# Pair sums of a Strassen-like down projection moved from accumulating DMAs to GpSimd, with new instruction orders around the stage

## The chip, the cores and the metric

One core of a Trainium2 chip runs the whole kernel. The metric is the device time of one execution in microseconds, as the median of the runs shown; lower is better. TensorE does the matmuls, VectorE (DVE), ScalarE (ACT) and GpSimd (POOL) the elementwise work, SyncE (SP) starts most DMAs.

## The reference, cut to what matters

```python
# x: 8 x 128 x 512 fp32 (1024 tokens), one LoRA index per batch row
gate = x @ W_gate.T + lora_gate(x)            # F = 1376, rank 16, scale 0.5
up   = x @ W_up.T   + lora_up(x)
act  = silu(gate) * up
c    = act @ W_down.T + lora_down(act)        # "first down projection", 512 out
nx   = c * rsqrt(mean(c*c) + 1e-5) * ln_w     # RMS norm
out  = x + (silu(nx @ g.T) * (nx @ u.T)) @ d.T   # I = 1792
```

## The kernel before

Every fp32 product is made of three fp32r matmuls: high part by high part, low by high, high by low. For each operand ACT writes the high part (a copy that rounds) and DVE then the low part (operand minus high part). So each operand costs one ACT copy and one DVE subtraction before TensorE may read it.

The large products are done in Winograd's form of Strassen's scheme: 2 x 2 blocks, seven products instead of eight, with sums of blocks as operands. The first down projection has the products 11, t2, 21, t3, t4, t1, 22, in this order on TensorE. `CDOWN` gives each its PSUM banks. Each has five items (`KC`), an item being three matmuls for each of two output tiles; 30 matmuls of 128 x 512 a product. The act operands of t2, t3, t4 and t1 are pair sums, made in place in the act buffer `act[:, tile, token half]`:

- t3: second half of tiles 0 to 4, plus the second half of tiles 5 to 9
- t2: first half of tiles 0 to 4, plus t3's operand
- t4: first half of tiles 5 to 9, plus t2's operand
- t1: t2's operand minus the operand of 22 (the second half of tiles 5 to 9)

Each sum overwrites a block, so it has to wait until the earlier product's operand has been split (`s_clo` counts the low parts made), and until the LoRA projection `t_c` on TensorE has read the tiles (`s_t`). The last tile's t3 and t2 sums are made by DVE (`last_pair_sums`). The weight operands of t2, t3, t1 and 22 are sums too: SP loads a block (`load_down_w`) and GpSimd starts accumulating DMAs on top (`add_w`, S2_21 to S4_11).

Engines run their instruction streams in order, and the order is written out by hand for each. What matters for the change:

- The loop over eight groups `j = 0..7` (`S1` is 8) makes gate and up: on TensorE q1, g, p4 of group j-1, p6, q2, p3, loras, p7. Beside it ACT does copies and silus (ca, cm, cu, cl), the high parts of the weights (`hi_a`, `hi_b`), the stack of LoRA factors (`stack_hi`) and `place_ad`, which `t_c` reads; DVE does `sums`, `lo_a`, `lo_b`, products and sums of results (c11, c12, c22_sum, c22_act, c21).
- `t_c` is done in three parts: before group 6, before group 7, and after product 11.
- `hi_w(p)`/`lo_w(p)` split the down weights of product p, `hi_c(p, n)`/`lo_c(p, n)` part n of its act operand (parts of one or two 512-element tiles). `seed`, `keep_u2`, `copy_u3`, `copy_p5` are ACT copies of PSUM banks between products that share partial results. `hi_w10`/`lo_w10` split the last weight rows and `hi_short`/`lo_short` the short last act tile, used by `short_c`.
- GpSimd makes the low weight parts of CT1 and C22 (`lo_w` in its block) and t1's subtraction; the pair sums of t3, t2 and t4 are seven DMAs from SBUF to SBUF that add (`add_act`).
- After product 22: `keep_y`, squares, `rsqrt`, `norm`, `scale` for token half 0 and then half 1 (`y_1`, last square), then q1(8), q1(9) with `sum_squares(1, .)` between, q2(8), and the FFN phase. `sums(G1+2)`, `sums(G1+3)` and their `hi_a`, `hi_b`, `lo_a`, `lo_b` prepare weights of the FFN's groups 10 and 11.

All elementwise work goes through helpers, so the profile shows their lines: L538 is any ACT copy, L1072 DVE's subtraction for a low part, L1202 its negated form, L1608 the group products, L1618 LoRA, L1838 `t_c`, L1863 the items of the down projection, L1877 `short_c`, L1884 the sums of squares.

Of the kernel before, what the change touches and what calls it, by code (L numbers as in the profile page):

```python
# [46 lines left out]
def build(nc, xT_in, idx_in, wsh_in, w0_in, wgu_in, wc_in, w10_in, vs_in, vj_in, agu_in, bgu_in, ad_in, bd_in, lnw_in, out):  # L47
# [2031 lines left out]
```

## Time and profile before

| what | value |
|---|---|
| median of 3 runs | 434.11 us (433.95 to 435.5) |
| profiled execution | 435.26 us, span 433.5 us |
| mean granted TensorE clock | 0.957 |
| busy: PE, DVE, ACT, POOL | 398.1, 330.9, 251.2, 36.8 us |
| idle PE time by line in the stage | L1863 t2: 8.2, t4: 4.9 and 1.1, 11: 4.1 us; L1884: 8.4 and 0.8 us |

The profile is of one execution; its span runs from the first to the last instruction, and the execution's own time is 1.8 us longer. An idle time in brackets stands before the first instruction of its row, with the engine that ended it.

### The profile page before, as it was taken

What the parts mean: (1) busy time and instruction counts of PE and PEld (TensorE: products, weight loads), DVE (VectorE), ACT (ScalarE), POOL (GpSimd) and SP (SyncE); (2) the same over time, 40 slices, a digit from 0 to 9 for tenths busy, and PEclk for the clock granted to TensorE, in tenths of its full rate; (3) what the DMA queues carried; (4) which work ended last, traced back from release to release, by engine and by line L of the source; (5) the groups of instructions that cost most, each with busy time, mean ns of one, the idle gap of its engine ahead of it and who ended that gap; (6) DMA issues with size and microseconds to landing.
All of it is one profiled execution on the core that took longest, in us unless ns stands there. A gap on an engine that the chain in (4) does not pass through costs nothing.

```text
span 433.5 us, 5739 instructions
## 1 busy us (share of the span) xinstructions
PE 398.1 (92%) x1954; PEld 328.1 (76%) x1954; DVE 330.9 (76%) x477; ACT 251.2 (58%) x389; POOL 36.8 (8%) x32
## 2 busy tenths in 40 slices
PE   9999999998996659779919999999999999999997
PEld 5988888886884547558817888888888888888885
DVE  4799987766538169276887988787978788899994
ACT  5889777677373069257355555556354559265730
POOL 6200000000012103840000000000000000000000
PEclk9999999998998959959977999999999999999999
DMA  7621252115679987700004001222223031504112
GB/s 254 195 86 34 88 143 73 48 50 166 140 170 237 249 206 126 164 2 0 0 0 147 0 1 50 97 64 82 97 81 115 2 133 52 177 2 170 62 48 98
DMA packets 17294, 42.37 MB, mean 98 GB/s; under 512 B 2546, under 2 KB 5106, under 8 KB 17266
## 3 DMA queue, kind: packets, MB, share of 16 engines
q1 hardware_dynamic: 13360, 32.19, 22.6%
q0 software_dynamic: 2784, 8.00, 10.1%
q10 hardware_dynamic: 1122, 1.84, 1.2%
q8 instruction: 15, 0.25, 0.2%
q14 instruction: 13, 0.11, 0.1%
HBM read 36.51 MB, written 2.10 MB: 89 GB/s over the span
## 4 chain that ended last, share of the span: by engine, by line
PE 65%; issue 13%; DMA 10%; DVE 6%; ACT 3%; POOL 2%; SPq 1%; POOLq 0%; DVEq 0%; ACTq 0%
PE bank L1608 41%; PE bank L1971 15%; DMA down_w_sums_raw<-wc_in 5%; PE bank L1863 3%; DVE xs L1072 2%; DMA act<-act 2%; PE bank L1618 2%; ACT stack L538 2%; DMA xa<-xT_in 1%; DMA wraw<-w_in 1%; PE bank L1802 1%; PE bank L1791 1%; POOL act L487 1%; POOL down_w_sums_raw L481 1%; DVE wx L1072 1%
## 5 line engine op out<-in xcount | busy, mean ns | idle before, releaser
L1608 PE MATMUL bank<-xs,ws 128*128 128x512 f32 x840 | 199.0, 395 | 2.9 <-ACT bank L538 1.9
L1608 PEld LDWEIGHTS bank<-xs,ws 128*128 128x128 f32 x840 | 158.9, 191 | 36.6 <-ACT bank L538 2.3
L538 ACT ACTIVATE xs<-act 128x512 fp32r<-128x512 f32 (+1 forms) x73 | 49.8, 702 | 42.0 <-DMA act<-act 14.2
L1072 DVE TENSOR_TENSOR xs<-act,xs 128x512 fp32r<-128x512 f32 (+1 forms) x66 | 53.4, 825 | 13.2 <-ACT xs L538 12.6
L1072 DVE TENSOR_TENSOR ws<-wraw,ws 128x256 fp32r<-128x256 f32 (+2 forms) x45 | 30.1, 670 | 20.1 <-ACT ws L538 20.0
L538 ACT ACTIVATE bank<-bank 128x512 f32<-128x512 f32 x34 | 19.4, 577 | 37.6 <-PE bank L1608 37.1
L1971 PE MATMUL bank<-xs,vs 128*128 128x512 f32 x168 | 38.2, 389 | 0.0
L1863 PE MATMUL bank<-xs,down_w_sums 128*128 128x512 f32 x120 | 30.5, 411 | 8.4 <-ACT bank L538 8.2
L538 ACT ACTIVATE mu<-bank 128x512 f32<-128x512 f32 x44 | 26.1, 596 | 18.2 <-PE bank L1608 12.8
L1971 PEld LDWEIGHTS bank<-xs,vs 128*128 128x128 f32 x168 | 31.5, 188 | 6.5
L1863 PE MATMUL bank<-xs,down_w 128*128 128x512 f32 x90 | 26.0, 449 | 10.1 <-issue 4.9
L1072 DVE TENSOR_TENSOR ws<-wsum,ws 128x1024 fp32r<-128x1024 f32 x20 | 24.5, 1225 | 13.3 <-ACT ws L538 13.3
L1863 PEld LDWEIGHTS bank<-xs,down_w_sums 128*128 128x128 f32 x120 | 23.7, 201 | 13.9 <-issue 9.0
L538 ACT ACTIVATE ws<-wraw 128x256 fp32r<-128x256 f32 (+2 forms) x44 | 26.8, 614 | 8.3 <-PE bank L1608 3.3
L1863 PEld LDWEIGHTS bank<-xs,down_w 128*128 128x128 f32 x90 | 19.1, 218 | 15.4 <-issue 9.6
L1971 PE MATMUL bank<-xs,ws 128*128 128x512 f32 x120 | 27.7, 389 | 0.0
L1971 PEld LDWEIGHTS bank<-xs,ws 128*128 128x128 f32 x120 | 22.5, 188 | 4.7
L538 ACT ACTIVATE stack<-bgu_raw 32x1024 fp32r<-32x1024 f32 (+1 forms) x20 | 22.8, 1138 | 0.3
L538 ACT ACTIVATE ws<-wsum 128x1024 fp32r<-128x1024 f32 x20 | 21.1, 1054 | 1.8 <-DVE wsum L1086 1.8
L610 ACT ACTIVATE act<-bank 128x512 f32<-128x512 f32 (+1 forms) x28 | 16.2, 592 | 8.2 <-PE bank L1618 5.7
L1608 PE MATMUL bank<-xs,wx 128*128 128x512 f32 x84 | 19.7, 389 | 0.0
L1608 PEld LDWEIGHTS bank<-xs,wx 128*128 128x128 f32 x84 | 15.8, 188 | 3.3
(146 smaller groups left out, 502.1 us busy)
## 6 DMA issues: line engine op xcount, KB each, us to landing
wraw<-wgu_in SPq DMA_DIRECT2D x22, 512.0 KB, 3.4
down_w_sums_raw<-wc_in POOLq DMA_DIRECT2D x7, 640.0 KB, 8.5
wdr<-vs_in SPq DMA_DIRECT2D x7, 512.0 KB, 3.3
wraw<-vj_in SPq DMA_DIRECT2D x3, 896.0 KB, 4.7
down_w_sums_raw<-wc_in SPq DMA_DIRECT2D x4, 640.0 KB, 4.7
act<-act POOLq DMA_DIRECT2D x4, 512.0 KB, 6.6
down_w_raw<-wc_in SPq DMA_DIRECT2D x3, 640.0 KB, 7.8
xa<-xT_in SPq DMA_DIRECT2D x4, 256.0 KB, 4.3
```

Of the source, the lines that this page charges most:

```text
L481: nc.gpsimd.dma_start(C_RAW[p], wc_in[i, j].rearrange("p (k m) -> p k m", k=KC), accum_op=ALU.add).then_inc(s_cw_add[n % 2], 16)
L487: nc.gpsimd.dma_start(to, more, accum_op=ALU.add).then_inc(s_t_add[n % 2], 16)
L538: return nc.scalar.activation(out_ap, in_ap, ACT.Copy, scale=scale)
L610: return nc.scalar.activation(out_ap, in_ap, ACT.Silu, scale=scale)
L1072: return nc.vector.tensor_tensor(out_ap, raw, v32(part), ALU.subtract)
L1608: ins = mm(z[:, :], w_slot(j)[:, w, s, k * P:(k + 1) * P], xs[:, c, r, k, :], start=(start and k == 0 and s == 0 and r == 0), stop=(k == 1 ...
L1618: ins = mm(z[0:m, half], stk[c % 2][:, 2 * t + q, cols], t_op[:, half], start=(alone and q == 0), stop=(q == 1), skip_group_check=True)
L1791: mm(UNIT_BANK[n][g][:, :], w0_tile(s, k, g, UNITS[n][0]), x_op(k, 1, r), start=(k == 0 and s == 0 and r == 0), stop=(k == KT - 1 and s == ...
L1802: ins = mm(SHORT_BANK[t][g][:, half], wsh[s][:, k, g, q, :], x_op(k, t, r)[:, half], start=(k == 0 and s == 0 and r == 0 and q == 0), stop ...
L1863: ins = mm(CDOWN[p][1][h][:, :], C_W[p][:, s, k, h * P:(h + 1) * P], slot_c(u, r), start=(p in (C11, CT1) and k == 0 and s == 0 and r == 0 ...
L1971: ins = mm(DOWN[p][3][h][:, :], down_w(i, s)[:, h * P:(h + 1) * P], slot_f(i, r), start=(p < 2 and k == 0 and s == 0 and r == 0), stop=(s ...
```

## The change

Seven things move or are replaced; the diff is cut to its core.

1. The seven `add_act` DMAs become `pair_sum`, a tensor_tensor on GpSimd, with one counter `s_tp` for all; t2's first two tiles are split as (0,1), (1,3), (3,4).
2. GpSimd no longer makes `lo_w(CT1)` and `lo_w(C22)`; DVE does. GpSimd makes the three `sums` of G1+3 instead of DVE.
3. `t_c` moves into the groups, between p4(j-1) and p6(j).
4. `stack_hi(4, 0)` and `(4, 1)` follow groups 4 and 5, `place_ad` follows group 5; `load_w(10)` is issued before the loads of the weights of 11 and t2.
5. `lo_w(C11)` goes from group 6 to an early place in group 7, and `lo_w(CT2)`/`hi_w(CT2)` behind t3's weights and t2's first operand.
6. In the down stage `hi_w(CT1)`, `hi_w(C22)`, the halves of w10, `place_td`, `copy_u3`, the table load, t3's and t4's operands get new places.
7. In the norm, half 1's first square is made by ACT, and the G1+2 and G1+3 weight work is spread to earlier and later places.

```diff
         CW_ORDER = (C11, CT2, CT3, C21, CT4, CT1, C22)
+        CW_HI = (C11, CT3, CT2, C21, CT4, CT1, C22)
...
-        S2_21, S2_22, S3_21, S1_21, S4_21, S4_22, S4_11 = range(7)
+        S2_21, S3_21, S2_22, S1_21, S4_21, S4_22, S4_11 = range(7)
...
-            for j in range(7, 10):
+            for j in range(7, 11):
                 load_w(j)
             sp.wait_ge(s_ad, 10)
             load_down_w(C11, 0, 0)
             sp.wait_ge(s_stklo, 10)
             load_down_w(CT2, 0, 0)
-            load_w(10)
...
-            def add_act(n, to, more):
-                if n >= 2:
-                    pool.wait_ge(*t_added(n - 2))
-                nc.gpsimd.dma_start(to, more, accum_op=ALU.add).then_inc(s_t_add[n % 2], 16)
-            def lo_w(p):
-                pool.wait_ge(s_cw_hi, CW_ORDER.index(p) + 1)
-                nc.gpsimd.tensor_tensor(C_W[p][:, 1], C_RAW[p], v32(C_W[p][:, 0]), ALU.subtract).then_inc(s_cw_lop, 1)
+            def pair_sum(to, more, op=ALU.add):
+                nc.gpsimd.tensor_tensor(to, to, more, op).then_inc(s_tp, 1)
+            def t2(k, end, done):
+                pool.wait_ge(s_clo, KC * C11 + end)
+                pool.wait_ge(s_tp, done)
+                pair_sum(act_c(k, end, 0), act_c(k, end, 1))
+            def t4(k, end):
+                pool.wait_ge(s_clo, KC * C21 + end)
+                pool.wait_ge(s_tp, T2_3)
+                pair_sum(act_c(KC + k, KC + end, 0), act_c(k, end, 0))
+            def t1(k, end):
+                pool.wait_ge(s_clo, KC * CT2 + end)
+                pool.wait_ge(s_tp, T4_4)
+                pair_sum(act_c(k, end, 0), act_c(KC + k, KC + end, 1), ALU.subtract)
             pool.wait_ge(*cw_loaded(CT2))
             add_w(S2_21, CT2, 1, 0)
...
             pool.wait_ge(s_t, 1)
+            pair_sum(act_c(0, 3, 1), act_c(KC, KC + 3, 1))
             pool.wait_ge(*cw_loaded(CT3))
             add_w(S3_21, CT3, 1, 0)
             pool.wait_ge(s_t, 2)
+            pair_sum(act_c(3, 4, 1), act_c(KC + 3, KC + 4, 1))
+            add_w(S2_22, CT2, 1, 1)
+            t2(0, 1, T3_012)
+            t2(1, 3, T3_012)
+            t2(3, 4, T3_3)
             pool.wait_ge(*cw_loaded(CT1))
             add_w(S1_21, CT1, 1, 0)
             pool.wait_ge(*cw_loaded(C22))
             add_w(S4_21, C22, 1, 0)
+            t4(0, 2)
+            t4(2, 4)
             pool.wait_ge(*cw_added(S4_21))
             add_w(S4_22, C22, 1, 1)
             pool.wait_ge(s_last, 2)
+            t4(4, 5)
+            t1(0, 1)
+            t1(1, 3)
             pool.wait_ge(*cw_added(S4_22))
             add_w(S4_11, C22, 0, 0)
+            t1(3, 5)
+            nc.gpsimd.tensor_tensor(wsum[:, 0:2, :], raw_w[:, 1::2, :], raw_w[:, 0:1, :].to_broadcast([P, 2, 256]),
...
+            nc.gpsimd.tensor_tensor(wsum[:, 3, :], wsum[:, 2, :], raw_w[:, 2, :], ALU.add).then_inc(s_wsum, 1)
...
             hi_c(C11, 2)
             hi_w(CT3, cw_added(S3_21))
             hi_c(CT2, 0)
+            hi_w(CT2, cw_added(S2_22))
             hi_c(CT2, 1)
+            hi_c(CT2, 2)
             hi_w(C21, cw_loaded(C21))
-            hi_c(CT2, 2)
...
+            hi_w(CT1, cw_added(S1_21))
             for n in range(3):
+                hi_c(CT4, n)
+            nc.scalar.preload_act_table(ACT.Abs_reciprocal_sqrt)
+            hi_c(CT1, 0)
             for i in range(2):
                 copy_u3(i)
+            hi_a(G1 + 2)
...
             sum_hi(0)
+            hi_w(C22, cw_added(S4_11))
             hi_c(C22, 1)
             hi_c(C22, 2)
+            rsqrt(0)
             for i in range(2):
                 copy_p5(i)
-            rsqrt(0)
             a.wait_ge(s_nx, 2)
             hi_x(1, X11, nx0[:, 0:2, :])
+            square(4)
+            square(5)
+            hi_a(G1 + 3)
+            square(6)
+            sum_hi(1)
             a.wait_ge(s_nx, 4)
             hi_x(1, X21, nx0[:, 2:4, :])
...
             square_hi()
+            hi_b(G1 + 3)
             ca(S1)
...
             lo_c(CT2, 0)
             c21(S1 - 1)
+            lo_w(CT2)
             lo_c(CT2, 1)
-            sums(G1 + 1)
+            lo_c(CT2, 2)
             lo_w(C21)
-            lo_c(CT2, 2)
             last_pair_sums()
             lo_c(CT2, 3)
             lo_c(C21, 0)
+            sums(G1 + 1)
             lo_c(C21, 1)
             lo_c(C21, 2)
+            lo_w10(0)
             lo_short(0)
             lo_w(CT4)
             lo_a(G1 + 1)
+            lo_c(CT3, 0)
+            lo_c(CT3, 1)
+            lo_w10(1)
+            lo_c(CT3, 2)
             lo_b(G1 + 1)
+            sums(G1 + 2)
+            lo_w(CT1)
             for n in range(3):
                 lo_c(CT4, n)
             lo_c(CT1, 0)
+            lo_a(G1 + 2)
             add_square(0, 1)
             lo_c(CT1, 1)
+            lo_b(G1 + 2)
...
             sum_lo(0)
+            lo_w(C22)
             lo_c(C22, 1)
             lo_c(C22, 2)
+            norm(0)
+            scale(0)
+            scale(1)
             y_1(0)
             y_1(1)
...
             lo_x(1, XF["11"], xs[:, X11, 1], nx0[:, 0:2, :], xs[:, X11, 0])
+            y_1(2)
+            add_square(1, 1)
+            add_square(1, 2)
+            sum_lo(1)
+            scale(2)
+            scale(3)
+            y_1(3)
+            last_square()
             lo_x(1, XF["21"], xs[:, X21, 1], nx0[:, 2:4, :], xs[:, X21, 0])
             lo_a(G1 + 3)
             norm(1)
...
             lo_t(1, 3)
+            lo_b(G1 + 3)
             c22_sum(S1)
...
                     if j > 0:
                         p4(j - 1)
+                    if j == S1 - 2:
+                        t_c(range(6))
+                    elif j == S1 - 1:
+                        t_c(range(6, 8))
                     p6(j)
```

## Rows read from the trace of the kernel before

**Rows 1.** Busy time by stage: window, then PE, PEld, DVE, ACT, POOL, PEclk.

```profile
97.00:133.00 36.00, 33.70 (x261) 27.34 (x259) 19.03 (x26) 21.63 (x38) 5.04 (x5) 0.95 0.65 151
133.00:160.00 27.00, 15.04 (x94) 12.05 (x95) 14.59 (x19) 8.26 (x16) 4.21 (x4) 0.76 1.01 263
160.00:190.00 30.00, 23.88 (x102) 18.90 (x100) 19.87 (x18) 21.12 (x28) 16.85 (x10) 0.90 0.57 108
190.00:233.00 43.00, 32.72 (x139) 26.70 (x140) 31.06 (x44) 19.22 (x26) 0.00 (x0) 0.82 0.08 28
233.00:433.50 200.50, 197.37 (x877) 163.43 (x875) 170.48 (x272) 107.51 (x180) 0.00 (x0) 1.00 0.22 74
```

**Rows 2.** Timeline of TensorE: start, duration, line, operation, count [idle before].

```profile
99.25 5.99 PE L1608 MATMUL bank<-xs,ws 128*128 128x512 f32 x18 [1.89 <-ACT bank L538]
...
107.28 2.83 PE L1838 MATMUL bank<-act,ad 128*32 128x128 f32 x96
...
114.47 4.27 PE L1608 MATMUL bank<-xs,ws 128*128 128x512 f32 x18
...
136.72 2.69 PE L1863 MATMUL bank<-xs,down_w 128*128 128x512 f32 x6 [4.12 <-DVE act L1147]
...
156.68 3.75 PE L1863 MATMUL bank<-xs,down_w_sums 128*128 128x512 f32 x8 [8.24 <-ACT bank L538]
...
186.03 2.90 PE L1863 MATMUL bank<-xs,down_w 128*128 128x512 f32 x6 [4.93 <-issue]
...
215.66 0.87 PE L1877 MATMUL bank<-xs,last_wd 128*128 128x256 f32 x6
...
227.58 0.76 PE L1884 MATMUL bank<-xs,ones 128*128 128x512 f32 x1 [8.37 <-ACT xs L538]
...
231.89 3.92 PE L1608 MATMUL bank<-xs,ws 128*128 128x512 f32 x15
```

**Rows 3.** Timeline of ACT.

```profile
92.19 4.30 ACT L538 ACTIVATE stack<-bgu_raw 32x1024 fp32r<-32x1024 f32 x4
96.51 2.21 ACT L538 ACTIVATE ad<-ad_raw 128x192 f32<-128x192 f32 x10
...
153.31 1.06 ACT L538 ACTIVATE xs<-act 128x1024 fp32r<-128x1024 f32 x1 [10.04 <-DMA act<-act]
...
182.72 1.27 ACT L538 ACTIVATE down_w_sums<-down_w_sums_raw 128x1280 fp32r<-128x1280 f32 x1 [7.83 <-DMA down_w_sums_raw<-wc_in]
```

**Rows 4.** Timeline of DVE.

```profile
133.40 1.49 DVE L1072 TENSOR_TENSOR down_w_sums<-down_w_sums_raw,down_w_sums 128x1280 fp32r<-128x1280 f32 x1
134.80 1.22 DVE L1072 TENSOR_TENSOR xs<-act,xs 128x1024 fp32r<-128x1024 f32 x1
135.93 0.68 DVE L1147 TENSOR_TENSOR act<-act,bank 128x512 f32<-128x512 f32 x1
...
185.03 4.95 DVE L1072 TENSOR_TENSOR xs<-act,xs 128x1024 fp32r<-128x1024 f32 x1 [8.82 <-ACT xs L538]
...
252.18 0.68 DVE L1134 TENSOR_TENSOR act<-mu,bank 128x512 f32<-128x512 f32 x1
```

**Rows 5.** DMA issues from 95 to 236 us: count, size each, median us to landing.

```profile
down_w_sums_raw<-wc_in POOLq DMA_DIRECT2D x7, 640.0 KB, 8.5
```

**Rows 6.** Timeline of issues: t2's weights on SP, the sum S2_21 on POOL.

```profile
99.12 0.42 SPq L348 DMA_DIRECT2D down_w_sums_raw<-wc_in  x1
...
104.45 1.05 POOL L481 DMA_DIRECT2D down_w_sums_raw<-wc_in  x1 [18.65 <-DMA down_w_sums_raw<-wc_in]
```

**Rows 7.** Groups of GpSimd instructions by shape: busy us, mean ns.

```profile
L491 POOL TENSOR_TENSOR down_w_sums<-down_w_sums_raw,down_w_sums 128x1280 fp32r<-128x1280 f32 x2 | 6.5, 3258 | 0.0
...
L532 POOL TENSOR_TENSOR act<-act 128x512 f32<-128x512 f32 x1 | 1.6, 1618 | 0.0
```

**Rows 8.** Timeline of GpSimd; L532 is t1's subtraction (512, 1024, 1024 elements).

```profile
179.80 6.21 POOL L532 TENSOR_TENSOR act<-act 128x512 f32<-128x512 f32 x3
185.66 3.23 POOL L491 TENSOR_TENSOR down_w_sums<-down_w_sums_raw,down_w_sums 128x1280 fp32r<-128x1280 f32 x1
```

More of the change, by code:

```diff
@@ L688, in hi_c @@
                 if name == "t2":
-                    for half in range(k // 2, (end - 1) // 2 + 1):
-                        a.wait_ge(*((s_last, 2) if half == 2 else t_added(T2_01 + half)))
+                    a.wait_ge(*((s_tp, T2_0 + n) if n < 3 else (s_last, 2)))
                 elif name == "t3":
-                    a.wait_ge(*t_added(T3_012 + k // 3))
+                    a.wait_ge(s_tp, (T3_012, T3_012, T3_3)[n])
                     if end == KC:
@@ L947, in _ @@
                     stack_rows(2, 0, slice(64, KS))
-                elif j < 4:
+                elif j < 6:
                     stack_hi(j // 2 + 2, j % 2)
-                elif j == 4:
-                    stack_hi(4, 0)
-                    stack_hi(4, 1)
-                    place_ad()
-                elif j == 5:
+                    if j == 5:
+                        place_ad()
+                elif j == 6:
                     hi_w(C11, cw_loaded(C11))
-                elif j == 6:
-                    hi_w(CT2, cw_added(S2_22))
             cl(S1 - 1)
@@ L979, in _ @@
                 keep_u2(i)
+            hi_c(CT3, 0)
+            hi_c(CT3, 1)
+            hi_w10(1)
+            hi_c(CT3, 2)
             hi_b(G1 + 1)
+            hi_w(CT1, cw_added(S1_21))
             for n in range(3):
-                hi_c(CT3, n)
-            hi_w(CT1, cw_added(S1_21))
-            hi_c(CT4, 0)
-            hi_w(C22, cw_added(S4_11))
-            hi_c(CT4, 1)
-            hi_c(CT4, 2)
+                hi_c(CT4, n)
+            nc.scalar.preload_act_table(ACT.Abs_reciprocal_sqrt)
+            hi_c(CT1, 0)
             for i in range(2):
                 copy_u3(i)
+            hi_a(G1 + 2)
             for m in range(2):
@@ L993, in _ @@
                 square(m)
-            hi_c(CT1, 0)
             hi_c(CT1, 1)
+            hi_b(G1 + 2)
             keep_y(2)
@@ L1422, in group @@
                     sums(w_of(w_next(j)))
+                if j == S1 - 1:
+                    lo_w(C11)
                 if j > S1 + 2 and j % 2 == 0:
@@ L1448, in group @@
                     lo_c(C11, 0)
-                    lo_w(CT2)
                     lo_c(C11, 1)
@@ L1714, in p7, with t_c, t_c_of_pairs @@
                 product(B_BANK[j % 2], j, WS3, XT3, False).then_inc(s_p7, 1)
+            def t_c(tiles):
+                for n in tiles:
+                    for t in range(2):
+                        for b in range(4):
+                            col = RANK * (b % 2)
+                            ins = mm(T_BANK[32 * b:32 * b + 32, t_cols(t, b)], ad[:, 2 * t + b // 2, n, col:col + 2 * RANK],
+                                     act_at(ORDER_C[n], t)[:, b * P:(b + 1) * P], start=(n == 0 and t == 0), stop=(n == FC - 1),
+                                     skip_group_check=True)
+                ins.then_inc(s_t, 1)
+            def t_c_of_pairs(end):
+                for done in (s_c11[1], s_c21[1], s_c12f, s_c22f):
+                    pe.wait_ge(done, end)
             def group(j):
```

147 lines of the change are left out of this document (38 added, 109 removed).

## Prediction

> **What bounds the kernel now.** I began with the busy table by stage [rows 1]. From 233 us on, TensorE is busy 197.4 of 200.5 us at full clock: nothing is to be won there without less work. Between 97 and 233 us it is busy 105.3 of 136 us, and at a mean clock below 1. That is the stage the change rearranges. The next view is TensorE's timeline of that stage [rows 2], where the reader should look for the idle time in brackets and for the duration of equal groups. The gaps are 1.89 us (before p6(5)), 4.12 (before the first item of 11), 8.24 (before t2), 4.93 (before t4) and 8.37 (before the squares' sum). After a gap the clock falls to 1.2 GHz and the same work takes longer: 18 matmuls took 5.99 us after the first gap and 4.27 in an unbroken stretch, 0.228 us each when warm.
>
> Then each gap's cause, from the other engines' timelines. ACT copies two stack halves (4.30 us) and places ad (2.21) before ca(5) [rows 3]: that is the 1.89. DVE makes lo_w(CT2) (1.49) before c11(7), which ends at 136.6 [rows 4]: part of the 4.12. ACT stands 10.04 us for the pair sum t2, an accumulating DMA, with the seed copies queued behind it [rows 3]: the 8.24. It stands 7.83 us for the last weight sum of 22, with copy_u3 behind it, the 4.93. The 8.37 lies in DVE's serial work for the norm. GpSimd's queue is the source of both DMA waits: an accumulating weight DMA takes 8.5 us from issue to landing [rows 5].
>
> **The change, part by part.** All positions are microseconds of the profiled execution before and of a walk through the new orders with the durations of the rows. DVE prices are 0.60, 1.14 and 1.41 us for 512, 1024 and 1280 elements back to back (durations less the 0.08 overlap of neighbours [rows 4]).
>
> *Stack halves and place_ad after group 5.* ACT does one half (2.15) after group 4, so ca(5) comes at 94.3 and p6(5) has no wait. The other half and place_ad, 4.4 us, fall into ACT's idle time after cl(5) and end at 107.0; t_c(range(6)), now behind p4(5), asks for ad at 107.7. Gain: 1.89 + (5.99 - 4.27) = 3.6, with rounding 3.8. t_c costs the same 2.83 in its new place [rows 2]. Last product of the loop: 132.6 to 128.8. If ad is later, TensorE waits by that much.
>
> *Loads.* load_w(10) now precedes the loads of 11 and t2, but the wait that bites is on place_ad: the load of t2's weights goes out at 107.4, not 99.1 [rows 6], and lands at 112.4. Behind it S2_21 is issued at 112.5 (before 104.45 [rows 6]), S3_21 at 119, S2_22 at 123.6 and lands at 132.6. Its readers hi_w and lo_w(CT2) are due about 142: 9 us of cover. It costs nothing, until a DMA is over 9 us late.
>
> *lo_w(C11) early, lo_w(CT2) late.* c11(7) no longer has a 1.4 us weight subtraction in front; with the product order it ends at 130.5, so the first item of 11 starts at 130.6 and the gap is 1.9 instead of 4.1.
>
> *Pair sums on GpSimd.* Seven DMAs of 6 to 8 us latency become eleven tensor_tensors (3 for t1 were there). Price: 512 elements took 1.62 us, 1280 took 3.26, and three in a row of 2560 elements 6.21, that is 2.4 ns an element [rows 7, 8]. The 1536-element one isn't in the trace: by 1.2 times the 1280 row 3.9; below, 3.26; above, 4.9 for three times 1.62. New sums: 2048 elements for t3, 2048 for t2, 2560 for t4, 2560 for t1 (as before) and 1024 for the weights of G1+3, some 24 us with starts. GpSimd has the time, so what matters is DVE. Here the trace has a warning: a 1024-element DVE subtraction with both inputs in SBUF, normally 1.22 us, took 4.95 at 185.03 [rows 4]. GpSimd was in a sum until 186.0 and in the next until 188.89 [rows 8], and DVE ended 1.1 after that. So I let such a DVE instruction wait until a string of GpSimd instructions ends, and GpSimd wait for a running DVE one. Bounds: no exclusion, 0; all 24 us on DVE's path, 24. I take, place by place, those that meet DVE's chain:
> - t2(0,1), (1,3), (3,4) become ready together at 129.9 and hold until 135.0. c12's last product stands behind them, and c22_sum(7) behind it: p4(7) starts at 136.4 (otherwise 133.3). With its 2.1 and lora at half clock, four items (5.5) and t_c (1.5) end at 145.8, against 148.4 before. Then t2 starts at once: its sums, weights (143.5) and seeds (144.9) are there, and t2 and 21 run unbroken to 159.7. The 10 us wait for the DMA is gone.
> - From the low part of 21's first operands (150.0) to that of t3's first, DVE has 7.9 us of work (three sums, two parts of 21, w10 half, short, lo_w(CT4), lo_a, one part), and GpSimd's t4(0,2), t4(2,4), then t4(4,5), t1(0,1), t1(1,3) hold it for 2.7 + 2.7 + 5.2 = 10.5. 150.0 + 7.9 + 10.5 = 168.4: t3 waits 8.7 us for DVE, and pays 2.8 for the clock (as before t2 now: 8 matmuls 3.75 instead of 1.8, and 0.9 in the next 24).
> - Then 8.6 us of DVE work, lo_w(CT1) (1.4, moved here from GpSimd) and t1(3,5)'s 2.7 stand before t4's first part: 179.7. TensorE is there at 168.4 + 6.9 + 2.8 + 1.4 = 179.5.
>
> *hi_w(C22) behind t1, lo_w(C22) on DVE.* copy_u3 no longer stands behind the DMA of 22: the sum S4_11 is issued near 168 and lands at 175, is read near 189. lo_w(C22)'s 1.4 lies in DVE's slack before 22 (weights at 190.5, used after 196). So t4, t1 and 22 run without a gap: 8.3 + 8.8 + 8.3 = 25.4 (30 matmuls of 0.228 and 12 short ones each, and the sum of squares). End 205.1, against 216.5 before [rows 2]. This is where t3's late start is paid back.
>
> *The norm.* Gone from DVE between copy_p5 and the squares are sums(G1+2) and (G1+3), two lo_a, two lo_b and first_square: 1.5 + 1.5 + 4.1 + 0.7 = 7.8; norm(0) and half the scaling run before 22 ends. What remains after the last short product is y_1(3), the last square, its low part (2.1) and lo_x (1.2): 208.4. TensorE's own q1(8), half q1(9) and three sums take it to 208.8. Before, q2(8) began at 231.89 + 0.68 = 232.6 [rows 2]. Gain: 23.8, of which 11.4 stood at the end of 22 and 12.4 come here.
>
> *lo_b(G1+3) late.* It is 1.2 us before c22_sum(8), which ended at 252.9, half a microsecond before its use [rows 4]; norm(1) starts 0.5 later relative to TensorE. Cost: 1.2 + 0.5 - 0.6 = 1.1.
>
> Sum: -23.8 + 1.1 = -22.7. The profiled execution took 435.26, 1.15 over the median of 434.11; the difference is laid on the median: 411.4. I say 412, since a walk overlooks small waits.
>
> **A rule on the port.** The row at 185.03 shows DVE shut out across two GpSimd instructions. The Trainium skill (SBUF — State Buffer, Who interferes with whom) says that a VectorE instruction with two SBUF inputs and a GpSimd one that reads SBUF exclude each other, whoever starts first holding the pair for its whole instruction. By that rule, the trace agrees with 4.95 us on the exclusion; it speaks of one instruction, not of a string.
>
> **Rivals.**
> *A. DVE gets in between two GpSimd instructions.* Against it is the 4.95 row, which is one case, where the second sum was queued already. Then p4(7) starts at 133.3 instead of 136.4; the later stretch keeps its sum of DVE and GpSimd time, from a start 3.1 earlier. 409.
> *B. The half clock lasts.* [rows 1] give 190 to 233 us a mean clock of 0.82 with short gaps. If waits scattered from 168 to 188 keep t3 and t4 at 1.2 GHz, their 60 matmuls of full-clock 0.228 cost up to 13.7 more, of which 2.8 is counted; I take 8: 420.
> *C. GpSimd becomes the bound, and it is slower.* If back-to-back DVE instructions shut GpSimd out as its string does DVE, the sums come late. t1's last part is due near 191, and ends in my walk near 176. Each microsecond beyond 15 of starvation counts; it turns slower past 15 + 22.7 = 38 us of starvation, say 40: 436.5. DVE was idle 22.5 us between 133 and 190 [rows 1] and GpSimd needs 18 there, which speaks against it.
> *D. Nothing gained* as the waits for data only move to t3. It takes 8.7 + 22.7 = 31 us of wait there; DVE's list has no such work. 434.
>
> **How the numbers follow.** Forecast 0.50, A 0.20, B 0.23, C 0.04, D 0.03. The forecast's own range is 407 to 416. 8 in 10 goes from 403 (A, with no exclusion at all in the t3 stretch: six less) to 425 (B with its whole price). Half a per cent is 2.2 us, about what a measurement can tell from none. Faster 0.93, same 0.03, slower 0.04.
>
> **What the new profile would show.** Right: no gap at p6(5); 1 to 3 us before the first item of 11; t2 without a wait; DVE subtractions of 3 to 6 us beside strings of GpSimd sums; the largest gap of the stage before t3, 6 to 10 us; none over 2 from t4 to q2(8); q2(8) near 209. Wrong: ACT waiting for t2's weight sum past 142; DVE subtractions at their usual length throughout (A); granted clock 0.5 throughout t4 (B); ACT waiting for t1's sums (C).

## The result and the profile after

The changed kernel took 415.38 us (median of 4, 413.85 to 415.83) against 434.03 (median of 4, 432.41 to 435.5): ratio 0.9565, interval 0.9522 to 0.9608. The forecast was 412, the range 403 to 425. The profiled execution took 414.94, span 412.9. Medians below are of the runs that are not in the slow state: 4 of the 9 runs of the kernel with the sums alone in the old orders, 1 of the 10 with added waits, and up to 3 of each set of the kernel before were slow and are left out.

Executions differ by about 1 us before anything that was changed: the first LoRA matmuls start between 26.7 and 27.7 us in the traces of this case. So I compare positions against a mark, the start of p4(4)'s LoRA matmuls (96.96 us before, 96.06 after). Here is TensorE's timeline of the changed kernel, to be read against [rows 2]. L1605 is now the group product, L1860 an item of the down projection, L1718 `t_c`, L1874 `short_c`, L1881 the sums of squares.

```profile
96.06 0.40 PE L1615 MATMUL bank<-tneg,stack 128*128 128x256 f32 x2
96.30 4.27 PE L1605 MATMUL bank<-xs,ws 128*128 128x512 f32 x18
...
106.91 2.83 PE L1718 MATMUL bank<-act,ad 128*32 128x128 f32 x96
...
117.89 3.06 PE L1605 MATMUL bank<-xs,ws 128*128 128x512 f32 x12 [0.39 <-DVE ws L1074]
...
127.04 1.55 PE L1605 MATMUL bank<-xs,ws 128*128 128x512 f32 x6
130.53 2.27 PE L1860 MATMUL bank<-xs,down_w 128*128 128x512 f32 x6 [1.94 <-DVE act L1149]
134.52 2.93 PE L1605 MATMUL bank<-xs,ws 128*128 128x512 f32 x6 [1.72 <-DVE mu L1133]
...
144.91 7.14 PE L1860 MATMUL bank<-xs,down_w_sums 128*128 128x512 f32 x30
151.88 6.96 PE L1860 MATMUL bank<-xs,down_w 128*128 128x512 f32 x30
168.39 8.88 PE L1860 MATMUL bank<-xs,down_w_sums 128*128 128x512 f32 x30 [9.54 <-DVE xs L1074]
...
178.54 3.59 PE L1860 MATMUL bank<-xs,down_w 128*128 128x512 f32 x15
...
203.15 0.88 PE L1874 MATMUL bank<-xs,last_wd 128*128 128x256 f32 x6
...
208.26 0.50 PE L1881 MATMUL bank<-xs,ones 128*128 128x512 f32 x1 [1.68 <-ACT xs L818]
209.06 0.50 PE L1881 MATMUL bank<-xs,ones 128*128 128x512 f32 x1 [0.30 <-DVE xs L1074]
209.40 5.24 PE L1605 MATMUL bank<-xs,ws 128*128 128x512 f32 x15
...
232.88 3.02 PE L1605 MATMUL bank<-xs,ws 128*128 128x512 f32 x12 [0.55 <-DVE act L1136]
```

The gaps of 1.89, 8.24, 4.93 and 8.37 us [rows 2] are gone. One of 9.54 has come before t3, and 1.7 to 2 us stand at three places. From the mark, in microseconds:

| place | before | after | gained so far | forecast |
|---|---|---|---|---|
| end of the loop's last product | 35.6 | 32.5 | 3.1 | 3.8 |
| end of `t_c`, start of t2's stage | 51.5 | 48.9 | 2.6 | 2.6 |
| start of t3 | 75.7 | 72.3 | 3.3 | 4.2 |
| start of t4 | 89.1 | 82.5 | 6.6 | 6.3 |
| end of 22 | 119.6 | 108.0 | 11.6 | 11.4 |
| start of p4(8) | 156.4 | 136.8 | 19.6 | 22.7 |

After p4(8) the two traces run alike: the spans differ by 20.6, of which 0.9 is the mark. Busy time by stage (columns as in [rows 1]; the last two are the DMA engines' share and GB/s) shows what became of DVE. It is busy 28.0 of 31 and 28.3 of 30 us where it was 14.6 of 27 and 19.9 of 30. By an estimate from the rows of the two windows, some 15 us of these 56.3 are time that instructions lasted beyond their undisturbed length, where it was 3.7 of 34.5 before; the rest of the difference is work that the new orders put here.

```profile
129.00:160.00 31.00, 26.59 (x146) 20.84 (x146) 27.98 (x26) 21.29 (x32) 16.18 (x10) 0.89 0.66 184
160.00:190.00 30.00, 21.61 (x98) 18.21 (x99) 28.29 (x24) 16.62 (x23) 12.47 (x7) 0.83 0.25 56
```

DVE's timeline shows it row by row (to compare with the 185.03 row of [rows 4]). The instructions have 1024, 512, 256, 1024, 1280, 768 and 512 elements; undisturbed they take 1.2, 0.7, 0.4, 1.2, 1.5, 1.0 and 0.7 us.

```profile
112.94 4.90 DVE L1074 TENSOR_TENSOR ws<-wsum,ws 128x1024 fp32r<-128x1024 f32 x1 [4.02 <-ACT ws L540]
...
131.06 2.81 DVE L1118 SCALAR_TENSOR_TENSOR act<-mu,act 128x512 f32<-128x512 f32 x1
...
150.05 2.52 DVE L1086 TENSOR_TENSOR wsum<-wsum,wraw 128x256 f32<-128x256 f32 x1
...
154.68 3.44 DVE L1074 TENSOR_TENSOR last_wd<-last_wd_raw,last_wd 128x1024 fp32r<-128x1024 f32 x1
...
159.74 2.55 DVE L1074 TENSOR_TENSOR down_w<-down_w_raw,down_w 128x1280 fp32r<-128x1280 f32 x1
162.21 3.09 DVE L1074 TENSOR_TENSOR ws<-wraw,ws 128x768 fp32r<-128x768 f32 x1
165.22 3.02 DVE L1074 TENSOR_TENSOR xs<-act,xs 128x512 fp32r<-128x512 f32 x1
```

Beside them stands GpSimd's timeline, as [rows 8]. L481 is `pair_sum`.

```profile
112.92 3.82 POOL L481 TENSOR_TENSOR act<-act 128x1536 f32<-128x1536 f32 x1
...
130.93 2.39 POOL L481 TENSOR_TENSOR act<-act 128x1024 f32<-128x1024 f32 x1
133.26 1.74 POOL L481 TENSOR_TENSOR act<-act 128x512 f32<-128x512 f32 x1
...
154.24 2.79 POOL L481 TENSOR_TENSOR act<-act 128x1024 f32<-128x1024 f32 x1 [1.96 <-DVE xs L1204]
...
157.59 1.68 POOL L481 TENSOR_TENSOR act<-act 128x512 f32<-128x512 f32 x1
159.41 1.53 POOL L481 TENSOR_TENSOR act<-act 128x512 f32<-128x512 f32 x1
160.90 3.58 POOL L481 TENSOR_TENSOR act<-act 128x1024 f32<-128x1024 f32 x1
...
165.05 2.64 POOL L481 TENSOR_TENSOR act<-act 128x1024 f32<-128x1024 f32 x1
```

A long DVE instruction ends about its own working time after a GpSimd sum's end: 112.94 ends at 117.84, the sum beside it at 116.74; 154.68 at 158.12, the sum at 157.03. It goes both ways: the sum of 1024 at 160.90 took 3.58 us instead of 2.4, while DVE's 1280 elements ran until 162.29. And DVE did get in between two sums (131.06 ran after the sum that ended at 133.32, while the one at 133.26 waited), which my forecast had not let it do.

### The profile page after: what moved, and what is told of

Same layout as the page of the kernel before. It is cut to its first block, busy times and chain, and to the rows that moved or that the text cites. A ratio compares the mean times of both kernels' runs of the same rounds, so it can differ in the third digit from the quotient of the medians.

```text
span 412.9 us, 5738 instructions
## 1 busy us (share of the span) xinstructions
PE 393.1 (95%) x1954; PEld 324.7 (79%) x1954; DVE 346.1 (84%) x475; ACT 252.3 (61%) x390; POOL 47.0 (11%) x34
## 4 chain that ended last, share of the span: by engine, by line
PE 83%; DVE 10%; issue 4%; ACT 3%; DVEq 0%; ACTq 0%
PE bank L1605 48%; PE bank L1968 16%; PE bank L1860 5%; PE bank L1823 3%; PE bank L1777 3%; DVE xs L1074 3%; PE bank L1812 3%; PE bank L1615 2%; DVE ws L1074 2%; ACT xs L540 1%; PE bank L1718 1%; PE bank L1771 1%; DVE last_wd L1074 1%; DVE down_w L1074 1%; DVE wsum L1086 1%
## 5 line engine op out<-in xcount | busy, mean ns | idle before, releaser
L1605 PE MATMUL bank<-xs,ws 128*128 128x512 f32 x840 | 198.7, 394 | 2.7 <-DVE mu L1133 1.7
L1605 PEld LDWEIGHTS bank<-xs,ws 128*128 128x128 f32 x840 | 158.0, 190 | 37.2 <-DVE mu L1133 2.4
L1074 DVE TENSOR_TENSOR ws<-wraw,ws 128x256 fp32r<-128x256 f32 (+2 forms) x45 | 32.2, 718 | 14.4 <-ACT ws L540 14.3
L1074 DVE TENSOR_TENSOR ws<-wsum,ws 128x1024 fp32r<-128x1024 f32 x20 | 28.2, 1409 | 16.6 <-ACT ws L540 16.6
L1860 PE MATMUL bank<-xs,down_w_sums 128*128 128x512 f32 x120 | 30.4, 410 | 9.5 <-DVE xs L1074 9.5
L1860 PEld LDWEIGHTS bank<-xs,down_w_sums 128*128 128x128 f32 x120 | 23.5, 199 | 15.1 <-issue 10.1
L481 POOL TENSOR_TENSOR act<-act 128x512 f32<-128x512 f32 (+2 forms) x11 | 26.3, 2401 | 14.8 <-DVE xs L1204 5.5
L1968 PE MATMUL bank<-xs,ws 128*128 128x512 f32 x120 | 27.7, 389 | 0.0
L1860 PE MATMUL bank<-xs,down_w 128*128 128x512 f32 x90 | 22.3, 402 | 1.9 <-DVE act L1149 1.9
L540 ACT ACTIVATE stack<-bgu_raw 32x1024 fp32r<-32x1024 f32 (+1 forms) x20 | 22.7, 1137 | 0.3
L1860 PEld LDWEIGHTS bank<-xs,down_w 128*128 128x128 f32 x90 | 17.1, 194 | 5.8 <-issue 2.3
L1605 PE MATMUL bank<-xs,wx 128*128 128x512 f32 x84 | 19.7, 389 | 0.0
```

The lines of the kernel that those rows point to most:

```text
L481: nc.gpsimd.tensor_tensor(to, to, more, op).then_inc(s_tp, 1)
L540: return nc.scalar.activation(out_ap, in_ap, ACT.Copy, scale=scale)
L1074: return nc.vector.tensor_tensor(out_ap, raw, v32(part), ALU.subtract)
L1605: ins = mm(z[:, :], w_slot(j)[:, w, s, k * P:(k + 1) * P], xs[:, c, r, k, :], start=(start and k == 0 and s == 0 and r == 0), stop=(k == 1 ...
L1860: ins = mm(CDOWN[p][1][h][:, :], C_W[p][:, s, k, h * P:(h + 1) * P], slot_c(u, r), start=(p in (C11, CT1) and k == 0 and s == 0 and r == 0 ...
L1968: ins = mm(DOWN[p][3][h][:, :], down_w(i, s)[:, h * P:(h + 1) * P], slot_f(i, r), start=(p < 2 and k == 0 and s == 0 and r == 0), stop=(s ...
```

## The experiments

Each comparison stands beside runs of the kernel before on the same chip; the ratio is to those, so that the sets can be set side by side. These medians of before are 434.03 us for the first row, 433.28 for the next four, 433.80 for the four behind them and 431.63 for the last three. A hundredth of the ratio is 4.3 us. A difference of two medians from different sets can be off by as much as these medians differ, so the ratios decide there.

| kernel | median us | ratio, interval |
|---|---|---|
| changed | 415.38 | 0.9565, 0.9522 to 0.9608 |
| t4, t1 sums on 16 columns | 402.75 | 0.9283, 0.9234 to 0.9333 |
| fills instead of those sums | 402.47 | 0.9285, 0.9218 to 0.9352 |
| t4, t1 sums on DVE | 406.79 | 0.9397, 0.9348 to 0.9447 |
| new orders, sums by DMA | 419.94 | 0.9697, 0.9648 to 0.9745 |
| sums on GpSimd, old orders | 436.43 | 1.0016, 0.9955 to 1.0077 |
| low weight parts on GpSimd | 419.08 | 0.9615, 0.9560 to 0.9669 |
| old norm section | 423.45 | 0.9707, 0.9648 to 0.9766 |
| DVE sums, scale(2) earlier | 406.48 | 0.9334, 0.9272 to 0.9397 |
| old orders, sums with waits | 430.23 | 0.9978, 0.9939 to 1.0016 |
| t2, t4, t1 sums on DVE | 404.61 | 0.9353, 0.9286 to 0.9420 |
| the same, two norm edits | 403.70 | 0.9330, 0.9263 to 0.9398 |

### What delays t3: the sums made narrow

The same edit stands in t4 (shown) and in t1.

```diff
-                pair_sum(act_c(KC + k, KC + end, 0), act_c(k, end, 0))
+                pair_sum(act_c(KC + k, KC + end, 0)[:, :, 0:16], act_c(k, end, 0)[:, :, 0:16])
...
```

> The sums of t4 and t1 are made on 16 of each 512 columns (the rest of those operands is left as it was), everything else as in the changed kernel. Theory port: DVE subtractions beside GpSimd sums wait for them; the DVE time lost between 149 and 168 us (2.1 + 2.2 + 1.1 + 1.1 + 2.2 + 2.3 us above the usual durations) is what delays t3. Then the gap before t3 falls from 9.5 to under 2 us, the half clock after it with it, and the time falls by 8 to 11 us. Rival list: DVE's own list before t3's first low part is too long, and the gap stays over 6 us with a time less than 3 us lower.

402.75 us, 12.6 below the changed kernel. No wait at all is left before t3. DVE's instructions have their usual lengths: the low part of w10's first half takes 1.28 us where it took 3.44. The list rival is out: without the neighbour, DVE's list reaches t3 in time. The gain is above the 8 to 11 I gave; 11.9 of it is there at the start of t4 (70.6 us from the mark for 82.5). The 9.5 us gap takes the half clock after it along: t3's 30 matmuls take 8.88 us after the gap, with a granted clock of 0.52 in their first 4 us, and 6.96 in this kernel.

### Reading or being there: fills instead of sums

```diff
+            def fill(to):
+                for i in range(2):
+                    fills.append(0)
+                    nc.gpsimd.memset(to, 0.5).then_inc(s_fill, 1)
+                    pool.wait_ge(s_fill, len(fills))
+                nc.gpsimd.memset(to, 0.5).then_inc(s_tp, 1)
...
-                pair_sum(act_c(KC + k, KC + end, 0), act_c(k, end, 0))
+                fill(act_c(KC + k, KC + end, 0))
```

> The sums of t4 and t1 are replaced by three fills of the same tiles each (GpSimd writes only, reads nothing; the operands are constants), about as long on GpSimd as the sums (3.0 for 2.7 us per 1024 elements). Theory port, reads exclude: DVE subtractions keep their usual 1.2 us and the time is that of the narrow sums, within 1 us. Rival, any GpSimd instruction excludes DVE, or the operands are simply late: the time is within 2 us of the changed kernel, gap before t3 7 us or more.

402.47 us, that of the narrow sums. GpSimd's timeline and DVE's in the fill kernel:

```profile
152.58 0.96 POOL L494 MEMSET act<- 128x1024 f32 x1
153.48 1.97 POOL L492 MEMSET act<- 128x1024 f32 x2
155.51 0.96 POOL L494 MEMSET act<- 128x1024 f32 x1
```

```profile
153.66 1.22 DVE L1084 TENSOR_TENSOR last_wd<-last_wd_raw,last_wd 128x1024 fp32r<-128x1024 f32 x1
154.80 0.68 DVE L1084 TENSOR_TENSOR xs<-act,xs 128x512 fp32r<-128x512 f32 x1
155.40 1.49 DVE L1084 TENSOR_TENSOR down_w<-down_w_raw,down_w 128x1280 fp32r<-128x1280 f32 x1
```

GpSimd is busy as long (2.9 us for t4's first two tiles, 2.79 for the sum), with the operands ready as late, but reads nothing, and DVE is not held. The fills are short instructions with waits between them, but that does not explain it: the DVE row at 153.66 lies wholly beside fills that run on from 153.48 to 155.45. So a GpSimd instruction that reads SBUF excludes a DVE instruction with two SBUF inputs, and one that only writes does not. The Trainium skill (SBUF — State Buffer, Who interferes with whom) has this rule, reads against two inputs and not against a pure write; these rows agree with it, 1.22 us beside a fill and 3.44 beside a sum.

### The sums on DVE

t4 is shown; t1 likewise. Both are gone from GpSimd; behind them stands DVE's new order, in which lo_w(CT1) and sums(G1 + 2) also move behind t4's parts. On ACT copy_u3 goes ahead of t1's first operand.

```diff
+            def t4(k, end):
+                v.wait_ge(s_clo, KC * C21 + end)
+                v.wait_ge(s_tp, T2_3)
+                to = act_c(KC + k, KC + end, 0)
+                nc.vector.tensor_tensor(to, to, act_c(k, end, 0), ALU.add).then_inc(s_tp, 1)
...
             lo_c(CT3, 1)
+            t4(0, 2)
+            t4(2, 4)
             lo_w10(1)
             lo_c(CT3, 2)
+            t4(4, 5)
             lo_b(G1 + 1)
-            sums(G1 + 2)
-            lo_w(CT1)
             for n in range(3):
                 lo_c(CT4, n)
+            lo_w(CT1)
+            t1(0, 1)
+            t1(1, 3)
+            t1(3, 5)
+            sums(G1 + 2)
```

> The sums of t4 and t1 are made by DVE (0.6 us per 512 elements, 5.8 us in all), behind t3's first two low parts and behind t4's parts; copy_u3 goes ahead of t1's first operand on ACT. Theory port: DVE loses less by making the sums (5.8 us) than by waiting for GpSimd (some 11 us), and most of them lie behind t3's start: gap before t3 under 2 us, 7 to 11 us faster than the changed kernel. Rival list: DVE is the bound up to t1, so what is gained before t3 is waited for before t4 or t1; less than 4 us faster.

406.79 us, 8.6 below the changed kernel (7.3 by the ratios, 0.9397 against 0.9565). The largest wait at t3 is 0.32 us. The moves of lo_w(CT1), sums(G1 + 2) and copy_u3 were not tried apart from the sums; the wait before t3, ahead of all three, fell as in the narrow kernel. Two t4 sums of 1024 took DVE 2.35 us together, where beside GpSimd's sums single subtractions had lost 2 us each. The part left on GpSimd, the weight sums of G1+3, shows the reverse exclusion. GpSimd's row, then DVE's:

```profile
176.12 5.03 POOL L513 TENSOR_TENSOR wsum<-wraw 128x512 f32<-128x512 f32 x1 [15.43 <-DVE wx L1057]
```

```profile
175.86 0.68 DVE L1292 TENSOR_TENSOR sqr<-sqr 128x512 f32<-128x512 f32 x1
176.46 2.35 DVE L1057 TENSOR_TENSOR xs<-act,xs 128x1024 fp32r<-128x1024 f32 x2
...
179.33 0.69 DVE L1057 TENSOR_TENSOR xs<-act,xs 128x512 fp32r<-128x512 f32 x1
```

A GpSimd sum of 512 elements needs about 1.3 us (1.29 in the row of t3's second sum of this trace) and this one took 5.03, while DVE ran five instructions back to back from 175.86 to 180.02.

### The two halves of the change, each without the other

The new orders with the accumulating DMAs, for all seven sums of t3, t2 and t4 as for this one, with `t_added()` as before:

```diff
-            pair_sum(act_c(0, 3, 1), act_c(KC, KC + 3, 1))
+            add_act(T3_012, act_c(0, 3, 1), act_c(KC, KC + 3, 1))
...
```

> The new orders with the seven accumulating DMAs back for the pair sums of t3, t2 and t4 (t1 stays on GpSimd). Theory: the replaced DMAs' latency was the wait before t2; with DMAs back in the new orders ACT waits again for t2's operand (6 to 8 us from issue, two in a row), t2 starts 5 to 9 us later, but DVE is freer for t3: in sum 2 to 8 us slower than the changed kernel. Rival orders: the new orders hide the DMA latency and the sums on GpSimd bring nothing; within 2 us, or faster by what the port costs (up to 8 us).

419.94 us: 4.6 above the changed kernel (5.7 by the ratios). TensorE's timeline of this kernel:

```profile
148.74 2.79 PE L1731 MATMUL bank<-act,ad 128*32 128x128 f32 x48 [8.79 <-issue]
156.57 8.95 PE L1873 MATMUL bank<-xs,down_w_sums 128*128 128x512 f32 x30 [5.05 <-DVE xs L1217]
...
184.19 5.26 PE L1873 MATMUL bank<-xs,down_w 128*128 128x512 f32 x15 [3.63 <-DVE xs L1087]
```

The DMA wait is there, 8.8 + 5.1 us in front of `t_c` and t2, as ACT stood 10.33 and 4.74 us for DMAs. t2 starts 11.8 us later from the mark than in the changed kernel, more than the 5 to 9 expected. In return t3 has no wait, but t4 has one of 3.63 us. So the sums on GpSimd exchange 13.8 us before t2 and 3.6 before t4 for 9.5 before t3.

And the sums alone, in the orders of before:

```diff
             def add_act(n, to, more):
-                if n >= 2:
-                    pool.wait_ge(*t_added(n - 2))
-                nc.gpsimd.dma_start(to, more, accum_op=ALU.add).then_inc(s_t_add[n % 2], 16)
+                nc.gpsimd.tensor_tensor(to, to, more, ALU.add).then_inc(s_t_add, 1)
```

> One part alone: the kernel before with its seven accumulating DMAs replaced by GpSimd sums of the same tiles; all orders as before. Theory: the 8.2 us wait for t2's operand goes, the 4.9 and 8.4 us waits before t4 and the squares stay (they belong to copy_u3 behind the weight sum and to the norm): 4 to 9 us faster than before. Rival orders alone carry the change: less than 2 us faster, since another wait takes the place.

No gain: ratio 1.0016. The reason I gave for a gain was half right. t2 does start without its 8.24 us wait, at 54.5 us from the mark instead of 59.7. But t3 waits 16.49 us. The first item of 11 waits 6.26 instead of 4.12, and the 4.93 us before t4, which I had expected to stay, are gone behind the late t3. The DVE, GpSimd and TensorE rows before t3, from an execution of 438.3 us:

```profile
170.00 12.70 DVE L1070 TENSOR_TENSOR ws<-wsum,ws 128x1024 fp32r<-128x1024 f32 x1
```

```profile
169.79 3.18 POOL L489 TENSOR_TENSOR down_w_sums<-down_w_sums_raw,down_w_sums 128x1280 fp32r<-128x1280 f32 x1
172.78 5.99 POOL L530 TENSOR_TENSOR act<-act 128x512 f32<-128x512 f32 x3
178.61 2.99 POOL L489 TENSOR_TENSOR down_w_sums<-down_w_sums_raw,down_w_sums 128x1280 fp32r<-128x1280 f32 x1
```

```profile
183.44 9.22 PE L1861 MATMUL bank<-xs,down_w_sums 128*128 128x512 f32 x30 [16.49 <-DVE xs L1070]
```

One subtraction of 1.2 us stood beside five GpSimd instructions and ended 1.1 us after the last (181.60). The nine executions of this kernel took 431.08 to 438.53 us, and two of them 431; whether DVE stood as long in those, no trace shows. In the kernel before, DVE was idle or held for 4.95 us there and nobody waited long for it; with the sums earlier, the same string meets DVE on t3's path.

### What lets DVE in

In the changed kernel DVE got in between two sums, here it did not through five. One difference shows in the rows. Here the GpSimd instructions start 0.16 us or more before the one ahead has ended (172.78 against 169.79 + 3.18 = 172.97, 178.61 against 178.77). Where DVE got in, they overlap by 0.06 or less (133.26 against 133.32). So a wait for its own completion behind each subtraction and each sum of GpSimd, in the kernel of the old orders:

```diff
                 nc.gpsimd.tensor_tensor(part, part, act_c(KC + k, KC + end, 1), ALU.subtract).then_inc(s_t1, 1)
+                pool.wait_ge(s_t1, n + 1)
...
```

> The kernel with the sums alone (all orders as before), and after each GpSimd sum and weight subtraction a wait for its own completion, so that the next one can't start 0.2 to 0.4 us before its end. There a DVE subtraction of 1024 elements stood 12.70 us beside five GpSimd instructions in a row. Theory gap: DVE is let in only where GpSimd leaves the port between two instructions; with the waits it gets in after the first one and takes under 5 us, t3 starts 6 to 9 us earlier and the kernel is 4 to 8 us faster than with the sums alone. Rival: GpSimd keeps the port while the next instruction is queued, whatever the overlap; 10 us or more again, and no difference in time.

```profile
168.00 4.40 DVE L1073 TENSOR_TENSOR ws<-wsum,ws 128x1024 fp32r<-128x1024 f32 x1
```

```profile
168.13 3.18 POOL L490 TENSOR_TENSOR down_w_sums<-down_w_sums_raw,down_w_sums 128x1280 fp32r<-128x1280 f32 x1
171.39 8.22 POOL L532 TENSOR_TENSOR act<-act 128x512 f32<-128x512 f32 x3
179.69 3.81 POOL L490 TENSOR_TENSOR down_w_sums<-down_w_sums_raw,down_w_sums 128x1280 fp32r<-128x1280 f32 x1
```

The same subtraction takes 4.40 us: it ran after the first GpSimd instruction. The one before it, 512 elements beside two t4 sums, falls from 4.75 to 3.52 us. The two engines take turns after that: GpSimd's three t1 parts now need 8.22 instead of 5.99. t3 starts at 77.9 us from the mark instead of 86.7, as the theory had it. A gain in time of 4 to 8 us is not shown: the median is 6.2 lower (430.23 to 436.43), but the ratios differ by 1.6 us only and their intervals overlap. So what the waits do to DVE is shown by one trace of each kernel. Why the strings of the changed kernel overlap less than these stays open.

### The low weight parts, the norm section

The two `lo_w` go back to GpSimd, the first behind t1's sums, the second behind the three weight sums, and are gone from DVE.

```diff
             t1(3, 5)
+            lo_w(CT1)
...
+            lo_w(C22)
...
```

> The changed kernel with lo_w of t1 and 22 back on GpSimd (behind t1's sums and behind the three weight sums). Theory: 1280 elements cost GpSimd 3.3 us each and block DVE's subtractions beside them, against 1.4 us of DVE itself; 22's weights are then ready later than needed (about 3 us after 192): 0 to 4 us slower. Rival: DVE is the bound before t4, so taking 1.4 us off its list gives time: 1 to 2 us faster.

419.08 us, 3.7 above the changed kernel by the medians, 2.2 by the ratios, whose intervals overlap: slower is likely, not shown. By position p4(8) starts 5.0 us later. 2.8 of this is t3's wait, 12.37 us instead of 9.54, 0.7 the clock behind it and 1.4 the norm section. The rows before t3 are another case of a string that DVE does not get into:

```profile
165.95 5.85 DVE L1080 TENSOR_TENSOR xs<-act,xs 128x512 fp32r<-128x512 f32 x1
```

```profile
165.77 2.64 POOL L485 TENSOR_TENSOR act<-act 128x1024 f32<-128x1024 f32 x1
168.19 3.04 POOL L482 TENSOR_TENSOR down_w_sums<-down_w_sums_raw,down_w_sums 128x1280 fp32r<-128x1280 f32 x1
```

The second starts 0.22 us before the first ends (168.41), and t3's first low part stands beside both, 5.85 us where it took 3.02 in the changed kernel. From t4's start to the end of 22 it is 25.5 us in both kernels: no late weights of 22, and no gain before t4, as the rival had it. Here 1.4 us of DVE is cheaper than 3.3 us of GpSimd that holds DVE.

The norm section as before, G1+2 and G1+3 again behind copy_p5 (ACT's order shown, DVE's likewise):

```diff
...
             rsqrt(0)
             a.wait_ge(s_nx, 2)
             hi_x(1, X11, nx0[:, 0:2, :])
             a.wait_ge(s_nx, 4)
             hi_x(1, X21, nx0[:, 2:4, :])
+            for j in range(G1 + 2, G1 + 4):
+                hi_a(j)
+                hi_b(j)
```

> The changed kernel with the norm section in the order of before: weight sums, hi and lo parts of G1+2 and G1+3 back between copy_p5 and the squares on DVE and ACT, none on GpSimd. My forecast gave the section 12.4 us less 1.1 later; by position the traces give 8.0 from the end of product 22 to p4(8). If the 8.0 is the section's own, this kernel is 7 to 10 us slower than the changed one. Rival: the section's gain was really DVE's earlier state (its list is lighter there now anyway), and it is less than 5 us slower.

423.45 us, 8.1 slower than the changed kernel (6.2 by the ratios), the wait of the kernel before in its old place:

```profile
216.30 0.77 PE L1871 MATMUL bank<-xs,ones 128*128 128x512 f32 x1 [8.37 <-ACT xs L529]
```

From the end of 22 to p4(8) it is 37.0 us here and 28.9 in the changed kernel, so the section's own worth is 8, and not the 11.3 of the forecast.

In the kernel with DVE's sums, `scale(2)` ahead of `sum_lo(1)`:

```diff
-            sum_lo(1)
             scale(2)
+            sum_lo(1)
             scale(3)
```

> Sums of t4 and t1 by DVE, and in the norm scale(2) ahead of sum_lo(1), in DVE's 0.7 us wait for ACT. The mis-sized term of my forecast is y_1(3), which waited for two scalings (start 206.5, its operand was there at 204.1). If that chain sets the 1.7 us gap at the squares' sum, it falls by 0.7, and the time by 0.7 to 1.5 against the kernel with the DVE sums alone. Rival: no difference that can be measured, since the scalings are needed for q2(8) anyway.

The wait before the last sum of squares falls from 1.72 to 1.06 us as expected, the median from 406.79 to 406.48: no difference that can be measured.

### Towards a faster kernel

t2's sums too go to DVE, behind c22_act(S1 - 1) (first part), and GpSimd's first t3 sum goes behind t3's weight sum (second part).

```diff
...
+            t2(0, 1, T3_3)
             lo_c(C11, 2)
+            t2(1, 3, T3_3)
+            t2(3, 4, T3_3)
             lo_w(CT3)
...
-            pool.wait_ge(s_t, 1)
-            pair_sum(act_c(0, 3, 1), act_c(KC, KC + 3, 1))
             pool.wait_ge(*cw_loaded(CT3))
             add_w(S3_21, CT3, 1, 0)
+            pool.wait_ge(s_t, 1)
+            pair_sum(act_c(0, 3, 1), act_c(KC, KC + 3, 1))
```

> The kernel with t4's and t1's sums on DVE, and now t2's too (1.7 + 0.6 us of DVE in place of 2.4 us of its waiting); GpSimd makes t3's first sum behind the next weight sum's issue, clear of lo_b(9). Theory: p4(7) loses its 2.35 us wait and g(7) its 0.15 to 0.6, DVE's load stays the same: 1 to 3 us faster than with t4's and t1's alone (406.8). Rival: DVE is the bound to t3 and t4 by now, and the wait moves there: within 1 us.

404.61 us. p4(7)'s wait is 0.27 us instead of 2.35, g(7)'s is gone; before and in t3 waits of 0.43 and 1.24 us have come (0.32 before). So of 2.4 us some 1.3 goes back to DVE's list: rival and theory both hold in part. In time the two kernels are not told apart: the ratios' intervals overlap.

The group product before the squares is no longer cut in two, and `scale(2)` stands ahead of `sum_lo(1)`:

```diff
                     sum_squares(1, 0)
-                    product(a_bank(j), j, W11, X11, True, range(1))
+                    product(a_bank(j), j, W11, X11, True).then_inc(s_q1, 1)
                     sum_squares(1, 1)
-                    product(a_bank(j), j, W11, X11, True, range(1, 2)).then_inc(s_q1, 1)
...
```

> All sums but t3's first two on DVE, scale(2) ahead of sum_lo(1), and TensorE's last sum of squares behind the whole of q1(9) instead of between its halves (0.7 us of work into a wait of 1.1 to 1.7). Expected 0.5 to 1.5 us under the kernel without the two norm edits, as the remaining wait before the squares falls to under 0.5 us. Rival: q2(8) waits for the low part of X21 instead, no difference.

403.70 us, ratio 0.9330, against 0.9565 for the changed kernel, with intervals apart. Against 404.61 it isn't shown to be faster. The wait before the squares became 0.40 + 0.30, and q2(8) now waits 0.73 for DVE, as the rival said.

## Why the prediction was right, and where it was off

**The number.** The forecast took 22.7 us off. By position 19.6 came. The profiled executions differ by 20.3, with the 0.9 of the mark, which no part of the change made; the medians differ by 18.65. What is missing by position, 3.1 us, lies in the norm section below (11.3 forecast, 8.0 measured); up to the end of 22 the sum came out 0.2 better than forecast, partly by luck.

**Loop end.** p6(5) has no gap and its 18 matmuls take 4.27 us; `t_c` found ad in place. 3.1 of 3.8 came. The 0.7 is g(7)'s 0.39 us wait for lo_b(9) with what follows from it: t3's first sum (112.92) and lo_b(9) (112.94) met, 4.90 us instead of 1.2. In the kernel with t2's sums on DVE, where they do not meet, this wait is gone and the loop ends at 31.8 us from the mark, which is the whole 3.8. I had seen GpSimd's long sum there, and left it out of the sum.

**Loads and weight sums.** No wait for t2's weight sum, as forecast. But hi_w(CT2) ran at 132.68 and not near 142, and S2_22, issued at 123.56, landed 6.0 us later: the cover was 3 us, not 9.

**Sums on GpSimd.** The price was right (1536 elements 3.82 us against 3.9). So was the point that GpSimd costs through DVE. The rule for it was wrong as a general one: I let a DVE instruction wait for a whole string, and here the engines took turns. At p4(7) this shows: 135.4 us on the old scale (134.52 + 0.9), between the forecast's 136.4 and rival A's 133.3. That `t_c` then ended where forecast is luck: p4(7)'s six matmuls took 2.93 us at a granted clock of 0.50, for the 2.1 in the sum. At t3 the rule's error is hidden as well. 168.4 was forecast, 169.3 measured on the old scale, and the gap was 9.5 for 8.7. The walk let five sums hold DVE for 10.5 us before t3 and put t1(3,5) behind it. The rows from 150.05 to 165.22 lasted 10.9 us beyond their usual lengths, beside six sums: t1(3,5) (165.05) held t3's first low part, and t4 found DVE ready. The narrow sums and the fills show that the gap is this exclusion.

**"The 10 us wait for the DMA is gone."** It is, but the two experiments on the halves show that the sentence gave the sums too much. In the old orders the sums gain nothing, in the new ones 4.6 us; the new orders without them 13.3 (419.94 against 433.28), some 18 together.

**t4 to the end of 22.** Forecast without a gap, found without a gap, 11.6 us gained for 11.4. That copy_u3 ahead of hi_w(C22) and DVE's lo_w(C22) in time make this is argued, and was not tried alone: with the two lo_w back on GpSimd the stretch took the same 25.5 us, and with the sums alone in the old orders the wait before t4 was gone too, hidden by t3's.

**The norm: the mis-sized term.** 12.4 - 1.1 = 11.3 was forecast, 8.0 came (19.6 - 11.6), and 8.1 was lost when the section was put back. The term is "what remains after the last short product": I took y_1(3) to run as soon as its product was there (204.0). DVE was 2.5 us behind: y_1(3) started at 206.51, behind the squares' sum, its low part and scale(2), (3), and ACT's square_hi at 207.59 behind the copy of X21. That is the 1.68 + 0.30 us wait. The clock did the rest: 15 matmuls at 209.40 took 5.24 us instead of 3.92 [rows 2], 1.3 more. The late lo_b(G1+3) cost 0.55 at p4(8), half of my 1.1. Together that is 2.7 of the 3.3 us; 0.6 isn't assigned. Moving scale(2) forward took 0.66 off the wait and nothing measurable off the time, so this account of the chain is read from rows and only in part tried.

**Rivals.** A's mechanism was there and gave no 3 us; of t3 and t4, B's half clock was in t3's first part alone (t4's 15 matmuls take 3.59, full speed); C did not occur in the changed kernel, though the 5.03 us of a 1.3 us sum beside DVE's string shows its mechanism exists.

## What to carry to other kernels

Before giving GpSimd an elementwise job beside a busy DVE, count it twice: a sum with SBUF inputs holds DVE's two-input instructions for its own length, which here was 2.4 us per 1024 elements where DVE itself needs 1.1. When an asynchronous transfer is replaced by an instruction, look at who was idle while the transfer ran: here the same replacement gave no gain in the old orders and 4.6 us in the new. In a walk through a serial chain, sum the engine's queue up to the instruction, not from when its operand is ready.

## What the hardware did that I had not expected

A DVE subtraction of 1.2 us lasted 12.70 us: where the next GpSimd instruction started 0.16 us or more before the end of the one ahead, DVE was not let in between them. So it was across two instructions in the kernel before (4.95, an overlap of 0.35) and with the low parts back (5.85, an overlap of 0.22), and across five here. A wait for its own completion behind each GpSimd instruction cut it to 4.40. The Trainium skill (SBUF — State Buffer, Who interferes with whom) speaks of the whole instruction; here the string of five was held as one, and the measurement decides. The other way, DVE's back-to-back instructions held a GpSimd sum of 1.3 us for 5.03.
